# Attention over feature pairs: scores reduced three steps at a time, with a fourth relu buffer and the low part written over the product

## The reference

```
e = jnp.stack([tbl_f[ids[:, f]] for all 33 f], axis=1)           # 1024 x 33 x 128
inner = x[:, row] * x[:, col]                                     # 1024 x 528 x 128
fm = jax.nn.relu(jnp.einsum('bpd,ad->bpa', inner, attn_W) + attn_b)
scores = jnp.einsum('ba,bpa->bp', gnn_feature, fm)
attn = jax.nn.softmax(scores, axis=1)
attn_output = jnp.einsum('bp,bpd->bd', attn, inner) * 100.0
h = jnp.concatenate([gnn_feature, attn_output, gnn_feature], axis=1)
h = jnp.maximum(h @ W_top1 + b_top1, 0.0)
h = jnp.maximum(h @ W_top2 + b_top2, 0.0)
y = h @ W_top3
```

## Time and profile before

| | us |
|---|---|
| median of 3 runs | 1272.69 (1272.43 to 1273.11) |
| the profiled execution | 1272.05 |
| its span in the trace | 1269.9 |
| PE busy | 1203.5 |
| DVE busy | 1153.3 |
| ACT busy | 1018.9 |

### The profile page before, as it was taken

The page is one execution under the profiler, slowest core; times in us unless marked ns, Lnnn a source line. Parts: engine busy times, 40 slices in busy tenths (PEclk is TensorE's granted clock), DMA queues, the critical chain, the costliest instruction groups (busy, mean ns, idle before and its releaser), DMA issues.

```text
span 1269.9 us, 21243 instructions
## 1 busy us (share of the span) xinstructions
PE 1203.5 (95%) x8732; PEld 898.6 (71%) x8732; DVE 1153.3 (91%) x649; ACT 1018.9 (80%) x1039; POOL 465.4 (37%) x270
## 2 busy tenths in 40 slices
PE   1499999999999999999999999999999999999998
PEld 1277777777777777777777777777777777777766
DVE  2399899998999989999899989999899998999994
ACT  1288898778987889878897798977888788887783
POOL 6586684018810388005850078201880000000000
PEclk9999999999999999999999999999999999999999
DMA  4212311311103111131101301031110300011001
GB/s 108 99 34 82 72 30 28 111 36 28 32 17 127 28 28 33 30 106 36 30 22 48 105 26 34 20 110 39 30 32 20 121 18 1 1 29 39 18 9 38
DMA packets 54863, 58.87 MB, mean 46 GB/s; under 512 B 10728, under 2 KB 49136, under 8 KB 53744
## 3 DMA queue, kind: packets, MB, share of 16 engines
q1 hardware_dynamic: 46304, 40.20, 10.5%
q0 software_dynamic: 8448, 17.32, 5.2%
q10 hardware_dynamic: 16, 0.00, 0.0%
HBM read 36.12 MB, written 17.31 MB: 42 GB/s over the span
## 4 chain that ended last, share of the span: by engine, by line
PE 77%; ACT 8%; issue 7%; DVE 6%; POOL 2%; DMA 0%; DVEq 0%; ACTq 0%; POOLq 0%
PE scores L607 18%; PE ring L577 16%; PE ring L584 12%; PE ring L585 11%; PE ring L586 11%; ACT fm L302 3%; PE ring L631 3%; DVE inner L413 3%; ACT inner_hi L310 3%; POOL x_rows L274 2%; PE ring L617 2%; DVE inner_lo L420 2%; PE ring L651 1%; ACT exp_pairs L317 1%; DVE attn L470 1%
## 5 line engine op out<-in xcount | busy, mean ns | idle before, releaser
L302 ACT ACTIVATE fm<-ring,attn_b_sb 128x848 f32<-128x848 f32 (+1 forms) x640 | 597.1, 971 | 184.9 <-PE ring L577 176.8
L413 DVE TENSOR_TENSOR inner<-xt 128x2112 f32<-128x2112 f32 x256 | 602.6, 2354 | 66.9 <-ACT xt L341 37.0
L274 POOL DMA_INDIRECT x_rows<-in_tbl,ids_all x264 | 464.7, 1760 | 489.0 <-PE ring L617 399.3
L420 DVE TENSOR_TENSOR inner_lo<-inner,inner_hi 128x1688 fp32r<-128x1688 f32 (+4 forms) x256 | 466.9, 1824 | 24.5 <-ACT inner_hi L310 21.6
L584 PE MATMUL ring<-inner_hi,attn_wt_lo 128*128 128x424 f32 (+1 forms) x971 | 434.4, 447 | 5.1 <-ACT fm L302 4.4
L310 ACT CAST inner_hi<-inner 128x1688 fp32r<-128x1688 f32 (+4 forms) x256 | 392.3, 1532 | 5.3 <-DVE inner L413 5.3
L585 PE MATMUL ring<-inner_lo,attn_wt_hi 128*128 128x424 f32 (+1 forms) x971 | 344.1, 354 | 0.0
L586 PE MATMUL ring<-inner_hi,attn_wt_hi 128*128 128x424 f32 (+1 forms) x971 | 344.0, 354 | 0.0
L577 PE MATMUL ring<-inner,attn_wt 128*128 128x424 f32 (+1 forms) x618 | 276.5, 543 | 10.2 <-issue 6.5
L607 PE MATMUL scores<-fm,gnn_blocks 128*32 128x264 f32 x4096 | 254.6, 389 | 6.3 <-ACT exp_pairs L317 6.3
L584 PEld LDWEIGHTS ring<-inner_hi,attn_wt_lo 128*128 128x128 f32 x971 | 182.8, 188 | 73.2 <-issue 39.0
(11 more groups left out here) (53 smaller groups left out, 204.7 us busy)
## 6 DMA issues: line engine op xcount, KB each, us to landing
x_dram<-x_rows SPq DMA_DIRECT2D x8, 2112.0 KB, 6.6
x_fields<-x_dram SPq DMA_DIRECT2D x128, 128.0 KB, 3.0
x_rows<-in_tbl,ids_all POOLq DMA_INDIRECT x264
attn_t<-attn_turned SPq DMA_DIRECT2D x124, 32.0 KB, 1.9
w_sb<-in_W_top SPq DMA_DIRECT2D x2, 512.0 KB
x_fields<-in_r_gnn_feature SPq DMA_DIRECT2D x1, 512.0 KB, 4.2
h<-in_W_top SPq DMA_DIRECT2D x1, 256.0 KB
ids_all<-in_ids SPq DMA_DIRECT2D x1, 132.0 KB, 2.8
```

The lines of the kernel that those rows point to most:

```text
L274: nc.gpsimd.indirect_dma_start(out=x_rows[:, f, :], out_offset=None, in_=tables[f], in_offset=bass.IndirectOffsetOnAxis(ap=ids_all[:, t, f ...
L302: nc.scalar.activation(dst, slot(("hidden", pair, j))[:, :, 0:n], ACT.Relu, bias=attn_b_sb[:, 0:1]).then_inc(s_fm, 1)
L413: nc.vector.tensor_tensor(dst, a, b, ALU.mult).then_inc(s_inner, 1)
L420: nc.vector.tensor_tensor(inner_lo[:, S % LO_BUFS, 0:COLS - at], inner[:, S % INNER_BUFS, at:], inner_hi[:, S % HI_BUFS, 0:COLS - at].bitc ...
```

## The change

Scores are reduced three steps in a run: the runs of a batch cover steps 0-2, 3-5, ..., 27-29 and 30-31, each after `hidden` of the step that follows its last, so a batch has 11 runs where it had 16. `fm` has four buffers, and the reduction is signalled for each step. The rest `inner_lo` no longer has a tile: it is written over the product it is taken from, through a second name (`low_parts`) for the same memory, and there are four product buffers. DVE's subtraction therefore no longer waits for a step's matmuls, and `product(S)` waits for all matmuls of step S-4. The activations of the MLP and its output row lie in the memory of `attn`, with a wait in `scale_attn` for an output transfer of earlier on.

```
-    INNER_BUFS, HI_BUFS, LO_BUFS, FM_BUFS = 3, 3, 2, 3
+    INNER_BUFS, HI_BUFS, FM_BUFS = 4, 3, 4
...
+    BATCH = [(S, min(S + 3, STEPS * (S // STEPS + 1))) for S in range(ALL) if S % STEPS % 3 == 0]
...
-        inner = sb("inner", [D, INNER_BUFS, COLS])
+        plain = sb("products", [D, INNER_BUFS, COLS])
+        inner = nc.alloc_sbuf_tensor_at("low_parts", [D, INNER_BUFS, COLS], FP32R, offset=nc.sbuf_base - INNER_BUFS * COLS * 4)
         inner_hi = sb("inner_hi", [D, HI_BUFS, SPLIT], FP32R)
-        inner_lo = sb("inner_lo", [D, LO_BUFS, SPLIT], FP32R)
...
+        spare = attn[:].rearrange("p a b -> p (a b)")
+        weighted = spare.rearrange("p (b f) -> p b f", f=I)
+        h1 = spare[:, 0:H1].rearrange("p (m b) -> p m b", b=P)
+        h2 = spare[:, H1:H1 + H2].rearrange("p (m b) -> p m b", b=P)
+        y_row = spare[0:1, H1 + H2:H1 + H2 + P]
...
                 if j == 0 and S >= FM_BUFS:
-                    act.wait_ge(s_red, (S - FM_BUFS) // 2 + 1)
+                    act.wait_ge(s_red, S - FM_BUFS + 1)
...
                 if p > 0:
                     act.wait_ge(s_pooled, FJ * p if p < T else FJ * T - 2)
+                    act.wait_ge(s_out, 16 * min(p, T - 1))
...
             def product(S):
                 if S >= INNER_BUFS:
-                    dve.wait_ge(s_lo, S - INNER_BUFS + 1)
-                    dve.wait_ge(s_hidden, CHUNKS * (S - INNER_BUFS) + NATIVE[S - INNER_BUFS])
+                    dve.wait_ge(s_hidden, CHUNKS * (S - INNER_BUFS + 1))
...
             def rest_of_inner(S):
-                dve.wait_ge(s_hi, S + 1)
-                if S >= LO_BUFS:
-                    dve.wait_ge(s_hidden, CHUNKS * (S - LO_BUFS + 1))
-                at = native_cols(S)
-                nc.vector.tensor_tensor(inner_lo[:, S % LO_BUFS, 0:COLS - at], inner[:, S % INNER_BUFS, at:],
-                                        inner_hi[:, S % HI_BUFS, 0:COLS - at].bitcast(FP32), ALU.subtract).then_inc(s_lo, 1)
+                dve.wait_ge(s_hi, split_steps(S))
+                at, end = native_cols(S), COLS
+                nc.vector.tensor_tensor(inner[:, S % INNER_BUFS, at:end], plain[:, S % INNER_BUFS, at:end],
+                                        inner_hi[:, S % HI_BUFS, 0:end - at].bitcast(FP32), ALU.subtract).then_inc(s_lo, 1)
...
-            def reduce_steps(S0, last_pair=False):
-                t, s0 = divmod(S0, STEPS)
-                if S0 in PART_END:
-                    pe.wait_ge(s_exp, PART_END.index(S0) + 1)
+            def relus_of(S):
+
+                return SLOTS * (S // 2) + (SLOTS if S % 2 else 3)
+
+            def reduce_steps(first, end):
+                t, s0 = divmod(first, STEPS)
+                if first in PART_END:
+                    pe.wait_ge(s_exp, PART_END.index(first) + 1)
...
-                pe.wait_ge(s_fm, SLOTS * (S0 // 2) + (3 if last_pair else SLOTS))
-                for S in (S0, S0 + 1):
-                    if last_pair and S > S0:
-                        pe.wait_ge(s_fm, SLOTS * (S0 // 2 + 1))
+                if end < ALL:
+                    pe.wait_ge(s_fm, relus_of(end - 1))
+                for S in range(first, end):
+                    if end == ALL:
+                        pe.wait_ge(s_fm, relus_of(S))
...
-                last.then_inc(s_red, 1)
+                    last.then_inc(s_red, 1)
...
-                if S >= 2 and S % 2 == 0:
-                    reduce_steps(S - 2)
-            reduce_steps(ALL - 2, True)
+                for first, end in BATCH:
+                    if end == S:
+                        reduce_steps(first, end)
+            reduce_steps(*BATCH[-1])
```

More of the change, by code:

```diff
@@ L44, in afm_tower @@
     NATIVE[0], NATIVE[1] = 4, 3
-    SPLIT = COLS - THIN
-    INNER_BUFS, HI_BUFS, LO_BUFS, FM_BUFS = 3, 3, 2, 3
+    FIRST = 0
+    SPLIT = COLS - min(EDGES[S % 2][NATIVE[S]] for S in range(ALL))
+    INNER_BUFS, HI_BUFS, FM_BUFS = 4, 3, 4
     RING = 3
@@ L59, in part_at @@
         return PART_END.index(S - after) if S - after in PART_END else None
+    BATCH = [(S, min(S + 3, STEPS * (S // STEPS + 1))) for S in range(ALL) if S % STEPS % 3 == 0]
+    assert set(PART_END) <= {end for _, end in BATCH}
     LAST_FIELDS_AT = (ALL - 3, ALL - 2)
@@ L131, in afm_tower @@
         attn_w_rows = x_fields[:, 1, 0, :]
-        weighted = attn[:].rearrange("p a b -> p (a b)").rearrange("p (b f) -> p b f", f=I)
-        weighted_tail = inner[:, 0, 0:QS * FN * I].rearrange("p (b f) -> p b f", f=I)
+        spare = attn[:].rearrange("p a b -> p (a b)")
[3 more added lines that the diff above has]
+        y_row = spare[0:1, H1 + H2:H1 + H2 + P]
+        weighted_tail = plain[:, 0, 0:QS * FN * I].rearrange("p (b f) -> p b f", f=I)
         ring = [pb(f"ring{i}", [P, 2, 512]) for i in range(RING)]
@@ L156, in afm_tower @@
         s_fm = sem("fm_ready")
-        s_red = sem("two_steps_reduced")
+        s_red = sem("steps_reduced")
         s_max = sem("max_ready")
@@ L194, in fields_in, with split_steps @@
             return min(FU, F - FU * c)
+        def split_steps(S):
+            return S - FIRST + 1
         def native_cols(S):
@@ L309, in round_inner @@
                 at = native_cols(S)
-                nc.scalar.copy(inner_hi[:, S % HI_BUFS, 0:COLS - at], inner[:, S % INNER_BUFS, at:]).then_inc(s_hi, 1)
+                nc.scalar.copy(inner_hi[:, S % HI_BUFS, 0:COLS - at], plain[:, S % INNER_BUFS, at:]).then_inc(s_hi, 1)
             def exps(p):
@@ L411, in product @@
                 b = bass.AP(tensor=b.tensor, offset=b.offset, ap=[part, sample, [1, K], field])
-                dst = inner[:, S % INNER_BUFS].rearrange("d (g k f) -> d g k f", g=GROUPS, k=K)
+                dst = plain[:, S % INNER_BUFS].rearrange("d (g k f) -> d g k f", g=GROUPS, k=K)
                 nc.vector.tensor_tensor(dst, a, b, ALU.mult).then_inc(s_inner, 1)
             def rest_of_inner(S):
-                dve.wait_ge(s_hi, S + 1)
-                if S >= LO_BUFS:
-                    dve.wait_ge(s_hidden, CHUNKS * (S - LO_BUFS + 1))
-                at = native_cols(S)
-                nc.vector.tensor_tensor(inner_lo[:, S % LO_BUFS, 0:COLS - at], inner[:, S % INNER_BUFS, at:],
-                                        inner_hi[:, S % HI_BUFS, 0:COLS - at].bitcast(FP32), ALU.subtract).then_inc(s_lo, 1)
+                dve.wait_ge(s_hi, split_steps(S))
+                at, end = native_cols(S), COLS
+                nc.vector.tensor_tensor(inner[:, S % INNER_BUFS, at:end], plain[:, S % INNER_BUFS, at:end],
+                                        inner_hi[:, S % HI_BUFS, 0:end - at].bitcast(FP32), ALU.subtract).then_inc(s_lo, 1)
             def gnn_block(t):
@@ L576, in hidden @@
                     if c < NATIVE[S]:
-                        nc.tensor.matmul(dst, attn_wt[:], inner[:, S % INNER_BUFS, begin:end], start=True, stop=True)\
+                        nc.tensor.matmul(dst, attn_wt[:], plain[:, S % INNER_BUFS, begin:end], start=True, stop=True)\
                             .then_inc(s_hidden, 1)
@@ L580, in hidden @@
                     if c == NATIVE[S]:
-                        pe.wait_ge(s_lo, S + 1)
+                        pe.wait_ge(s_lo, split_steps(S))
                     at = begin - native_cols(S)
-                    hi, lo = inner_hi[:, S % HI_BUFS, at:at + end - begin], inner_lo[:, S % LO_BUFS, at:at + end - begin]
+                    hi, lo = inner_hi[:, S % HI_BUFS, at:at + end - begin], inner[:, S % INNER_BUFS, begin:end]
                     nc.tensor.matmul(dst, attn_wt_lo[:], hi, start=True, stop=False)
```

7 lines of the change are left out of this document (2 added, 5 removed).

## The result

The changed kernel takes 1294.85 us (median of 6, 1294.68 to 1295.0) against 1272.34 us for the kernel before, measured beside it: a ratio of 1.0177, 95% interval 1.0166 to 1.0187. It is slower, by 22.5 us; 1291 was forecast. Its traced span is 1292.5 us where it was 1269.9.

A forecast was written before the change was run, and what follows sets the result against it. PE at 95% was first suspect, with ACT lagging at 3.65 us a step against PE's 3.02. Middle batches +16.2, first +3.7 and last -1.0 made +18.9 on 1272.05: 1291 us forecast, 0.65 for 1280 to 1300.

The forecast's parts named there:

- the first three: L593's relu waits 50 us or more; 0.4 to 0.8 gaps before third steps' last pairs; scores' exponentials wait gone.
- ACT's lag and the ring: Three hidden steps in a row: PE outruns ACT and stops for PSUM ring slots; ring alone +1.9 us a batch.
- Fewer runs: PE's runs of scores: 16 a batch become 11, 40 fewer at 0.285 us each, 11.4 us less work.
- The exponentials' wait: PE's wait of about 0.8 us, eight times, goes (6 to 7 us); step 3 stops 1.40 instead.
- DVE: Low part late by 0.45 in step 6, weighted sums' slots late after steps 7 and 13: +0.8 us a batch.
- The fourth product buffer: DVE's product buffers: the low parts' lead, which PE waits for, does not grow with the fourth buffer.
- In place: DVE's low part written over its own input: taken as 0, range 0 to 0.1 us each.
- First and last batch: Batches outside the six middle ones: first +3.7 us, last -1.0 us.
- The ring holds: Rival at PE's ring: ACT's lag is absorbed and both gains stay, 1255 us, up to 3 less; chance 0.14.
- DVE falls behind: Rival on DVE: in-place subtraction costs 0.1 us each, 1309 us, or DVE's bound of 1.9 a batch, 1299; chance 0.08.
- Half and half: Rival: ring stops come out at half the sum beyond the savings, 1268 to 1279 us; chance 0.13.
- the first rival: ACT's lag is absorbed, for instance by a relu overtaking, so PE keeps both gains: 1255 us; chance 0.14.

The follow-up runs named there:

- e6: Changed kernel with runs of one step, except the first of each batch and of the last part, which are of two: 1289.67 us, ratio 1.0140 to the kernel before.
- e2: Changed kernel with three product buffers in place of four, runs of three kept: 1340.11 us, ratio 1.0559 to the kernel before.
- e3: Changed kernel with ACT's rounding moved behind the step's relus in steps 2, 5, 8 and so on: 1295.42 us, ratio 1.0206 to the kernel before.
- e8: Changed kernel with ACT's rounding moved behind the step's relus and copies in steps 26 and 29 alone: 1297.09 us, ratio 1.0195 to the kernel before.
- e1: Changed kernel with runs of two steps again, new buffers and in-place low part kept: 1267.16 us, ratio 0.9983 to the kernel before.
- e7: As e5, with runs of three in steps 24 to 29 too and the rounding of steps 26 and 29 late: 1282.05 us, ratio 1.0078.
- e4: Changed kernel with runs of three for steps 0 to 17 of a batch and of two for the rest: 1266.79 us, ratio 0.9983.
- e5: As e4, but the first batch in runs of two throughout: 1267.65 us, ratio 0.9965 to the kernel before.
- e11: As e5, but runs of two also for steps 0 to 5, so threes only in steps 6 to 17: 1264.97 us, ratio 0.9963.

## Why the prediction was right

Time and mechanism came out as forecast: 1294.85 us for 1291. The marks that were to show it right are in the profile after: the first three, a batch of 153.2 us for 153, DVE's share of 89% for 91%, a run of three of 2.81 us. The forecast was +18.9 us and the span grew by 22.6. Of the 3.7 missing, 0.9 are in the middle batches, 1.3 in the first and 1.4 in the last. That the middle ones fit so closely is partly luck: two errors of opposite sign, below.

*ACT's lag and the ring.* Right, in sum and place. The stretches forecast and measured: steps 1-3 13.6 and 13.70; 4-6 12.8 and 12.92; 7-15 42.05 and 42.2; 16-18 14.8 and 14.88; 19-24 34.4 and 34.63; 25-27 13.7 and 13.77; 28-30 12.8 and 12.91; 31-0 8.2 and 8.22. Each is too short, mostly by 0.1, and the sum by 0.9. Two mis-sized terms explain most. The middle step of such a row takes 3.12 us (339.13 to 342.25 in the profile after), where I had counted 3.02. And a run is 0.325 (e6), not 0.285: that is 0.04 for each of 11 runs, 0.4 us.

*Fewer runs.* Right in kind. By e6 it is 40 x 0.325 = 13 us of PE's work, and none of it is seen in the total, since the stops are larger.

*The exponentials' wait.* Right: no row of it is left, and step 3 stops instead. In PE's timeline this is a gap of 1.24:

```profile
366.66 0.46 PE L593 MATMUL ring<-inner_hi,attn_wt_lo 128*128 128x424 f32 x1 [1.24 <-ACT fm L313]
```

*DVE: right in step 6, mis-sized behind it.* I had found step 6 reaching its low part 0.45 late, in place of its ring stop. It does, here in PE's rows and DVE's:

```profile
377.07 0.87 PE L586 MATMUL ring<-products,attn_wt 128*128 128x424 f32 x2
378.12 0.46 PE L593 MATMUL ring<-inner_hi,attn_wt_lo 128*128 128x424 f32 x1 [0.18 <-DVE low_parts L429]
...
378.62 0.35 PE L595 MATMUL ring<-inner_hi,attn_wt_hi 128*128 128x424 f32 x1
```

```profile
376.17 1.90 DVE L429 TENSOR_TENSOR low_parts<-products,inner_hi 128x1688 fp32r<-128x1688 f32 x1
```

The last matmul of the first split chunk starts 1.55 behind the native chunk, where in step 30 it is 1.10 (342.25 to 343.35). The 0.8 us a batch were for slots of the weighted sums that come free late, 0.35 behind step 7 and 0.5 behind step 13. Steps 7-9 and 13-15 are longer than I had them without that by less than 0.1 each. So this term was about 0.1, and the ring's 2.8 in place of 1.9: two errors of opposite sign. That DVE stands near it is shown by e2, e3 and e8, each of which makes low parts later and pays at once.

*The fourth product buffer.* I had said that the lead of the low parts doesn't grow with it. That holds where DVE waits for the rounding, 81.6 us in all. What I hadn't said is that runs of three need it: without it the ratio is 1.0559 for 1.0177 (e2), some 48 us more.

*In place.* Right: 256 low parts take 467.5 us, mean 1827 ns, where they took 466.9 and 1824.

```profile
L429 DVE TENSOR_TENSOR low_parts<-products,inner_hi 128x1688 fp32r<-128x1688 f32 (+4 forms) x256 | 467.5, 1827 | 81.7 <-ACT inner_hi L321 81.6
```

*First and last batch.* 5.0 and 0.4 measured for 3.7 and -1.0. In the first, steps 0-18 are longer by 2.3 where I had 1.4, steps 19-24 by 0.9 (0.8), steps 25 to the next 0 by 1.7 (1.5). The term that was wrong is what I took off for steps with two native chunks: steps 7-12, two of them such steps, went from 24.7 to 25.5 us, the full 0.8 of six plain steps. In the last, steps 1-18 are shorter by 0.8, steps 19-24 longer by 0.6 and the rest longer by 0.6, where my sum reads -0.4 + 0.2 - 0.8: I took too much off for the end. Neither was tested by itself.

*The rivals.* "The ring holds" falls with the stops in the timeline and with e1. "DVE falls behind", by an in-place cost, falls with the row above. "Half and half" falls with the ring's 2.8 us a batch for my 1.9. That reordering would free the slots, a thought of the first rival ("a relu could overtake"), is true where DVE can follow: in steps 4-15 of e3's first batch the rows of three then beat runs of two. In the middle batches e3, e7 and e8 lose the gain to late low parts. Not tried: late rounding in the first batch alone, and a ring with a fourth slot, the direct test of the slots.

## What to carry to other kernels

Before work on a busy engine is grouped to save switches, ask who catches up while it runs: here, in stretches without other jobs, the scores were the time in which ACT drained the PSUM ring, and a row of three steps (PE 3.02 us each, ACT 3.65) outran three slots. Compare each neighbour's work with the stretch between two such pauses, not with the whole loop. A buffer helps only at the queue that is full: more SBUF buffers couldn't help at a PSUM slot. Putting the helper's slot-freeing work first can remove the stop, but what it puts off makes the next engine late: it pays only if that engine has slack (e3, first batch and middle ones). Grouping pays where other jobs give the helper its time, as in steps 7 to 18 (e4, e5, e11), though little: 149.6 us a batch for 150.0 (e1).

## What the hardware showed that was not expected

In e8 PE was idle for 2.39 us near the end, waiting for a small transfer, and the granted clock then fell for some microseconds. These are its windows: us, busy us (instructions) of PE, PEld, DVE, ACT and POOL, granted clock, DMA share, GB/s.

```profile
1256.00:1258.00 2.00, 0.19 (x2) 0.00 (x0) 2.00 (x2) 2.00 (x3) 0.00 (x0) 1.00 0.22 57
1258.00:1260.00 2.00, 1.42 (x9) 1.45 (x10) 1.94 (x2) 0.78 (x1) 0.00 (x0) 0.80 0.23 60
1260.00:1262.00 2.00, 2.00 (x10) 1.92 (x9) 0.92 (x2) 0.00 (x0) 0.00 (x0) 0.50 0.08 18
1262.00:1264.00 2.00, 2.00 (x9) 1.50 (x8) 1.97 (x2) 0.41 (x1) 0.00 (x0) 0.85 0.44 132
1264.00:1266.00 2.00, 2.00 (x15) 1.98 (x14) 0.31 (x1) 1.52 (x2) 0.00 (x0) 1.00 0.67 163
```

The clock is at half, 1.2 of 2.4 GHz, in the third window, and full again in the fifth. The 16 matmuls behind the gap took 3.21 us in place of 1.95:

```profile
1258.58 3.21 PE L648 MATMUL ring<-attn_t,x_fields 128*128 128x128 f32 x16 [2.39 <-DMA attn_t<-attn_turned]
...
1265.12 1.95 PE L648 MATMUL ring<-attn_t,x_fields 128*128 128x128 f32 x16
```

That is part of why e8's last batch is 3.5 us longer than the changed kernel's. The ring's stops in the changed kernel, 1.3 us at most, had no such effect, the clock stayed at 1.00 there. In e2 shorter stops than e8's did, and not each time. In step 6 of every batch but the first PE stands about 1.7 us for a low part. In one batch, and in the next:

```profile
702.12 0.46 PE L593 MATMUL ring<-inner_hi,attn_wt_lo 128*128 128x424 f32 x1 [1.69 <-DVE low_parts L429]
...
861.05 0.46 PE L593 MATMUL ring<-inner_hi,attn_wt_lo 128*128 128x424 f32 x1 [1.67 <-DVE low_parts L429]
```

The windows behind the first stay at a granted clock of 1.00, those behind the second don't:

```profile
863.00:865.00 2.00, 2.00 (x9) 1.28 (x12) 2.00 (x2) 2.00 (x3) 0.00 (x0) 0.50 0.00 0
```

Steps 4-6 take 14.3 us in the four middle batches of the first kind and 15.8 in the two of the second; the last batch is of the second kind too. A stop of PE can so cost more than its own length, here 1.5 us more. The stops themselves differ by 0.04 us at most, so their length alone doesn't say whether the clock falls.
